# Rank-2 additions of a two-step pair placed in four row groups of the array, in a feed-forward with repeated weights

## What is computed

```python
def _qlora_linear(x, wq, A, B):          # rank r = 2, scaling 0.5
    w = jnp.tile(wq, (1, 4))
    return x @ w.T + x @ A.T @ B.T * LORA_SCALING
...
s = silu(x @ w_gate.T)                   # first feed-forward, I = 2752
# the half of each token's s with the smallest absolute value is set to zero
x = _layernorm(x + (s * (x @ w_up.T)) @ w_down.T)
...
gate = jax.nn.silu(_qlora_linear(x, w1q, a1, b1))    # second feed-forward
up = _qlora_linear(x, w3q, a3, b3)
return _layernorm(x + _qlora_linear(gate * up, w2q, a2, b2))
```

## Time and profile before

| | |
|---|---|
| median of three runs | 2139.07 us |
| the profiled execution | 2140.85 us |
| its span in the profile | 2139.1 us |
| TensorE matmul (PE) busy | 2047.8 us, 96%, 11008 matmuls |
| weight loads (PEld) busy | 1824.7 us, 85% |
| VectorE (DVE) busy | 1110.8 us, 52% |
| ScalarE (ACT) busy | 782.3 us, 37% |
| GpSimd (POOL) busy | 1055.7 us, 49% |
| mean granted clock of TensorE | 0.975 |

### The profile page before, as it was taken

One profiled execution on the slowest core, in us unless ns is written; L12 is line 12 of the kernel. 1 busy time (PEld: TensorE's weight loads), 2 busy tenths in 40 slices (PEclk: granted clock), 3 DMA queues, 4 the chain that ended last, 5 costly groups with the idle time before them and its releaser, 6 DMA issues.

```text
span 2139.1 us, 32155 instructions
## 1 busy us (share of the span) xinstructions
PE 2047.8 (96%) x11008; PEld 1824.7 (85%) x11008; DVE 1110.8 (52%) x1818; ACT 782.3 (37%) x1280; POOL 1055.7 (49%) x740
## 2 busy tenths in 40 slices
PE   8997959999999999999999999999998999999998
PEld 8997949978899998889999888998776777777776
DVE  1146773368965345896633488652025354354543
ACT  3245333355233334623232372322243415244251
POOL 6445744435444543454454345443575727366281
PEclk9998979989999998999999899999999999999999
DMA  4332313323443332344343234334431403314130
GB/s 132 93 94 66 104 44 92 93 72 97 137 127 110 109 93 70 97 138 126 88 132 93 70 95 140 108 111 139 132 121 46 157 30 124 102 49 147 50 127 40
DMA packets 90366, 213.63 MB, mean 100 GB/s; under 512 B 10360, under 2 KB 12408, under 8 KB 89188
## 3 DMA queue, kind: packets, MB, share of 16 engines
q1 hardware_dynamic: 85616, 194.97, 30.1%
q10 hardware_dynamic: 4608, 16.78, 2.0%
HBM read 194.93 MB, written 16.78 MB: 99 GB/s over the span
## 4 chain that ended last, share of the span: by engine, by line
issue 38%; PE 32%; POOL 25%; ACT 2%; DMA 1%; DVE 1%; POOLq 1%; SPq 0%; DVEq 0%; ACTq 0%
POOL wl L463 18%; PE bank L1277 10%; PE bank L1278 10%; PE bank L1279 10%; POOL w13l L463 3%; POOL h2l L561 2%; POOL xTl L463 1%; PE bank L1448 1%; PE bank L1410 1%; ACT junka L663 1%; POOL hql L567 1%; DMA w_in_place<-in_wd 1%; PE bank L1401 0%; PE bank L1420 0%; DMA w_in_place<-in_wu 0%
## 5 line engine op out<-in xcount | busy, mean ns | idle before, releaser
L463 POOL TENSOR_TENSOR wl<-w_in_place,wh 128x688 fp32r<-128x688 f32 (+1 forms) x432 | 676.5, 1568 | 795.8 <-ACT wh L604 795.6
L1277 PE MATMUL bank<-wh,xTh 128*128 128x344 f32 x2048 | 661.5, 323 | 31.5 <-POOL wl L463 15.6
L1279 PE MATMUL bank<-wh,xTl 128*128 128x344 f32 x2048 | 658.6, 322 | 0.0
L1278 PE MATMUL bank<-wl,xTh 128*128 128x344 f32 x2048 | 657.3, 321 | 0.0
L604 ACT CAST wh<-w_in_place 128x688 fp32r<-128x688 f32 (+1 forms) x432 | 305.1, 706 | 872.0 <-DMA w_in_place<-in_wu 310.9
L1277 PEld LDWEIGHTS bank<-wh,xTh 128*128 128x128 f32 x2048 | 388.2, 190 | 34.4 <-issue 21.0
L1278 PEld LDWEIGHTS bank<-wl,xTh 128*128 128x128 f32 x2048 | 388.4, 190 | 0.0
L1279 PEld LDWEIGHTS bank<-wh,xTl 128*128 128x128 f32 x2048 | 387.9, 189 | 0.0
L1277 PE MATMUL bank<-wh,hTh 128*128 128x512 f32 (+1 forms) x704 | 284.6, 404 | 12.2 <-ACT v L633 6.4
L1278 PE MATMUL bank<-wl,hTh 128*128 128x512 f32 (+1 forms) x704 | 282.9, 402 | 0.0
L1279 PE MATMUL bank<-wh,hTl 128*128 128x512 f32 (+1 forms) x704 | 282.5, 401 | 0.0
(11 more groups left out here) (130 smaller groups left out, 2456.0 us busy)
## 6 DMA issues: line engine op xcount, KB each, us to landing
w_in_place<-in_wg SPq DMA_DIRECT2D x128, 344.0 KB, 3.0
w_in_place<-in_wu SPq DMA_DIRECT2D x128, 344.0 KB, 3.0
w_in_place<-in_wd SPq DMA_DIRECT2D x168, 256.0 KB, 2.6
w_in_place<-in_w SPq DMA_DIRECT2D x90, 256.0 KB, 3.6
x_in_place<-in_xT SPq DMA_DIRECT2D x32, 256.0 KB, 3.5
y<-in_xtok SPq DMA_DIRECT2D x4, 2048.0 KB, 8.5
x<-y ACTq DMA_DIRECT2D x16, 512.0 KB, 3.5
xa<-x SPq DMA_DIRECT2D x16, 512.0 KB, 4.8
```

Source lines behind the costliest of these rows:

```text
L463: nc.gpsimd.tensor_tensor(lo, landed, hi.bitcast(F32), ALU.subtract).then_inc(done, 1)
L1277: nc.tensor.matmul(dst, ah, bh, start=start, stop=False)
L1278: nc.tensor.matmul(dst, ah, bl, start=False, stop=False)
L1279: return nc.tensor.matmul(dst, al, bh, start=False, stop=stop)
```

## The change

The four rank-2 additions of two steps (gate and up of each) become four matmuls that contract over six rows each, at rows 0, 32, 64 and 96, in four banks. Each group of six rows holds what the 96-row form held in three places: `b` high with `x` high, the low part of the one with the high part of the other, and the reverse. For this `a13s` gets 102 columns, so that bank 7 holds all the copies; `braw` gets all the copies of `b1` and `b3`; two masks of one column each, `split_b` and `split_x`, turn copies into high or low parts. The steps run in pairs: base matmuls of step m0 and m0 + 1, then the four additions, then the four `low_h` matmuls of the pair before. ScalarE and GpSimd follow the same order. The last pair's `low_h` moves into `down_2`, behind five chunks of both halves of group 0. `t2s` moves in memory.

```diff
@@ load_b, SyncE @@
                 for g in range(3):
-                    for i, (src, c0) in enumerate(((b1, 0), (b3, 0), (b2, IB), (b2, IB))):
-                        r0 = 32 * g + R * (i % 2)
-                        sp.dma_start(braw[r0:r0 + R, c0:c0 + src.shape[1]], src).then_inc(b_in, 16)
+                    for i, src in enumerate((b1, b3, b1, b3)):
+                        r0 = UP * i + R * g
+                        sp.dma_start(braw[r0:r0 + R, 0:IB], src).then_inc(b_in, 16)
+                    for i in range(2):
+                        r0 = 32 * g + R * i
+                        sp.dma_start(braw[r0:r0 + R, IB:IB + H], b2).then_inc(b_in, 16)
@@ GpSimd, last down @@
                 if d == 4:
...
-                    nc.gpsimd.memset(keep[:], 1.0).then_inc(pool_s, 1)
...
+                    for part, new, old, n in ((split_b, (LORA, -1.0), (0.0, 1.0), 2 * R), (split_x, (1.0, -1.0), (0.0, 1.0), R)):
+                        for i in range(2):
+                            fill(part[:, i:i + 1], old[i])
+                            for p0 in QUAD:
+                                fill(part[p0:p0 + n + R, i:i + 1], new[i])
+                                fill(part[p0:p0 + n, i:i + 1], old[i])
+                    pool.sem_inc(split_ready, 1)
                     nc.gpsimd.memset(t2s[0:LR, :].bitcast(F32), 0.0).then_inc(keep_ready, 1)
...
-                if d == 28:
...
-                    nc.gpsimd.memset(lg[0:LR, :].bitcast(F32), 0.0).then_inc(keep_ready, 1)
-                    nc.gpsimd.memset(lu[0:LR, :].bitcast(F32), 0.0).then_inc(keep_ready, 1)
@@ steps_2, GpSimd @@
-                for m in range(STEPS):
+                for m in range(0, STEPS, 2):
                     c, q, _ = place(m)
                     if c < CQ - 1:
                         low_13(b, c + 1, q)
-                    if m:
-                        low_h(m - 1)
+                        low_13(b, c + 1, q + 1)
                     if q == 0 and c:
                         low_q(c - 1)
-                    if m == 5:
+                    low_h(m)
+                    low_h(m + 1)
+                    if m == 4:
                         inv_std(NB + b - 1)
-                low_h(STEPS - 1)
                 low_q(CQ - 1)
@@ steps_2, ScalarE @@
+                for m in range(0, STEPS, 2):
+                    c, q, rows = place(m)
+                    if c < CQ - 1:
+                        high_13(b, c + 1, q)
+                        high_13(b, c + 1, q + 1)
+                    silu(m)
+                    silu(m + 1)
                     if q == 0 and c:
                         high_q(c - 1)
+                    high_h(m)
+                    high_h(m + 1)
@@ VectorE, preparation @@
             dve.wait_ge(b_ready, 2)
-            V.scalar_tensor_tensor(out=b13[64:LR, :], in0=braw[64:LR, 0:IB], scalar=LORA,
-                                   in1=b13[64:LR, :].bitcast(F32), op0=ALU.mult, op1=ALU.subtract).then_inc(b_ready, 1)
+            dve.wait_ge(split_ready, 1)
+            step(V.tensor_scalar(braw[0:LX, 0:IB], braw[0:LX, 0:IB], split_b[0:LX, 0:1], None, ALU.mult))
+            st.done()
+            V.scalar_tensor_tensor(out=b13[0:LX, :], in0=b13[0:LX, :].bitcast(F32), scalar=split_b[0:LX, 1:2],
+                                   in1=braw[0:LX, 0:IB], op0=ALU.mult, op1=ALU.add).then_inc(b_ready, 1)
@@ low_rank_x, VectorE @@
-                step(V.tensor_copy(th[0:n, :], banks[7][0:n, :]))
+                step(V.tensor_copy(lx[0:LX, :], banks[7][0:LX, :]))
+                step(V.tensor_scalar(rest[0:LX, :], banks[7][0:LX, :], split_x[0:LX, 0:1], None, ALU.mult))
                 st.done()
-                step(V.tensor_tensor(tl[0:n, :], banks[7][0:n, :], th[0:n, :].bitcast(F32), ALU.subtract))
-                st.done()
-                for i, dst in enumerate((lg, lu)):
-                    for p0, src in ((0, th), (32, tl), (64, th)):
-                        step(V.tensor_scalar(dst[p0:p0 + n, :], src[0:n, :].bitcast(F32), keep[0:n, i:i + 1], None,
-                                             ALU.mult))
+                step(V.scalar_tensor_tensor(out=lx[0:LX, :], in0=lx[0:LX, :].bitcast(F32), scalar=split_x[0:LX, 1:2],
+                                            in1=rest[0:LX, :], op0=ALU.mult, op1=ALU.add))
@@ steps_2, TensorE @@
+                for m0 in range(0, STEPS, 2):
...
+                    for m in (m0, m0 + 1):
...
+                        for i in range(2):
+                            dst = banks[2 * (m - m0) + i][0:rows, :]
+                            if m >= 2:
+                                pe.wait_ge((s_done, h_done)[i], STEPS * b + m - 1)
...
+                    for m in (m0, m0 + 1):
+                        mm = slice(c * Q4 * P + place(m)[1] * rows, c * Q4 * P + (place(m)[1] + 1) * rows)
+                        for i, done in enumerate((gg_done, uu_done)):
+                            p0 = QUAD[2 * (m - m0) + i]
+                            nc.tensor.matmul(banks[2 * (m - m0) + i][0:rows, :], b13[p0:p0 + 3 * R, mm],
+                                             lx[p0:p0 + 3 * R, :], start=False, stop=True).then_inc(done, 1)
+                    if m0:
+                        low_h(b, m0 - 2, q + 2 == steps_of(c))
+                        low_h(b, m0 - 1, False)
@@ down_2, TensorE @@
                 if t == 0:
+                    pe.wait_ge(h_done, STEPS * b + STEPS - 1)
...
+                    for n in range(2):
+                        for c in range(CQ - 1):
+                            add(n, c)
+                        if n == 0 and between is not None:
+                            between()
+                    low_h(b, STEPS - 2, False)
+                    low_h(b, STEPS - 1, False)
+                    pe.wait_ge(ql_done, CQ * (b + 1))
...
+                    for n in range(2):
+                        add(n, CQ - 1)
```

More of the change, by code:

```diff
@@ L1428, in steps_2 @@
                 pe.wait_ge(l_ready, b + 1)
-                for m in range(STEPS):
-                    c, q, rows = place(m)
+                for m0 in range(0, STEPS, 2):
+                    c, q, rows = place(m0)
                     if q == 0:
@@ L1455, in down_2, with add @@
+            def down_2(b, t, between=None):
+                tt = slice(t * P, (t + 1) * P)
+                def add(n, c):
+                    rows, w = rows_of(c), slice(n * 512, (n + 1) * 512)
+                    three(banks[2 * (t % 2) + n][:, :], hqh[0:rows, c, tt], hql[0:rows, c, tt], w2h[0:rows, c, w],
+                          w2l[0:rows, c, w], c == 0, False)
                 if t == 0:
+                    pe.wait_ge(h_done, STEPS * b + STEPS - 1)
+                    pe.sem_inc(passed_pe, 1)
@@ new lines, in down_2 @@
+                    low_h(b, STEPS - 2, False)
+                    low_h(b, STEPS - 1, False)
+                    pe.wait_ge(ql_done, CQ * (b + 1))
+                    pe.sem_inc(passed_pe, 1)
+                    for n in range(2):
+                        add(n, CQ - 1)
+                else:
+                    if t >= 2:
+                        pe.wait_ge(e_evac, 2 * NT * b + 2 * (t - 1))
+                        pe.sem_inc(passed_pe, 1)
+                    for n in range(2):
+                        for c in range(CQ):
+                            add(n, c)
+                        if n == 0 and between is not None:
+                            between()
```

96 lines of the change are left out of this document (35 added, 61 removed).

## The result

The changed kernel takes 2157.18 us (median of four runs, 2156.33 to 2160.12) against 2139.64 (four runs of the kernel before beside it, 2138.78 to 2142.1): a ratio of 1.0083, with a 95% interval of 1.0065 to 1.0100. It is 17.5 us slower, where 5.7 were forecast. The profiled executions are 2160.12 and 2140.85 us, with spans of 2158.3 and 2139.1, so the profiles differ by 19.2.

A forecast was written before the change was run, and what follows sets the result against it. TensorE was taken as the bound, GpSimd close behind. Four blocks -1.7, `down_2` +5.0, `low_rank_x` -2.4 and -0.7, last `down` +5.55 sum to +5.75 us on 2139.07: 2144.8 us, range 2132 to 2155.

The forecast's parts named there:

- d: How late the first of a pair's four additions starts on TensorE; taken as 0.17 us, between 0 and 0.26.
- Q: Time from a pair's first addition to its first `low_h` on TensorE; taken as 0.45 us, between 0.24 and 0.8.
- A's clean share: Rival: the additions share the array at no extra cost (d = 0, Q = 0.24), total 2138.7 us; chance 0.27.
- D's serial loads: Rival: the additions' loads follow one another and the array empties twice (Q = 0.8), total 2155.3 us; chance 0.11.
- E: Rival: the four additions run one after another (Q = 0.93), total 2149.7 us; chance 0.08.
- The pair and the chunk: Second feed-forward: a free pair of steps takes 7.12 us, chunks 2 and 3 14.87 each, limited by GpSimd's chain.
- T: Start of a pair's additions on TensorE, from which the prediction counted its times in us.
- Chunk 1: Normalization of the block before delays the second product and the root adds 1.0 us; next chunk at T + 10.9.
- `down_2`: Last two `low_h` stand later, so the rank-2 addition waits 1.24 us for `t2s`, four times: +5.0 us.
- `low_rank_x`: Three operations replace eight: TensorE's wait at block 0 falls from 4.86 to 2.45 us, -2.4; other three borders -0.7.
- The last `down`: First feed-forward's preparation: fills +1.65 us, six more transfers +1.8, a longer pass over `braw` +2.1; together +5.55.
- Rival C: TensorE stays the bound throughout, 44 pairs x 3 slots = -30.6 us, total 2116 us; chance 0.05.

The follow-up runs named there:

- one_group: The changed kernel with all four additions of a pair reading rows 0 to 5, so three add the wrong part: 2161.92 us, one run.
- stats_early: The changed kernel with layer-norm sums taken within the first two chunks and GpSimd's inverse root at step 6, ahead of that pair's low parts: 2141.26 us, ratio 0.9998.
- wait_3: stats_early with GpSimd writing zeros over zeros in `t2s` twice, ahead of `w13l` for chunk 2, as a deliberate delay: 2162.19 us, ratio 1.0087.
- lowh_mid: The changed kernel with a block's last two `low_h` moved between the halves of the first tile of `down_2`: 2153.61 us, ratio 1.0054.
- before_18: The kernel before the change with 18 transfers for b instead of 12, the six more to rows nothing reads: 2148.97 us, ratio 1.0038.
- root_only: The changed kernel with only GpSimd's inverse root moved to step 6, VectorE's sums left in steps 1 to 4: 2147.68 us, ratio 1.0032.
- prep_spread: The changed kernel with its 18 transfers for b in three groups of six, ahead of pieces 23, 25 and 26: 2152.36 us, ratio 1.0047.
- all_moves: The changed kernel with the edits of hq_first, lowh_mid, stats_early and prep_spread together: 2118.24 us, ratio 0.9891.
- hq_first: The changed kernel with ScalarE's `high_q` ahead of the pair's two Silus instead of behind them: 2151.79 us, ratio 1.0050.

## Why the prediction was wrong

The sign and the main mechanism were right: TensorE gains by the additions, GpSimd's chain of each pair takes it back. The size was wrong, 17.5 us instead of 5.7, and beyond the range's end of 2155.

1. **The additions** (d = 0.17, Q = 0.45 forecast): 0.09 and 0.43 to 0.44. Right; A's clean share (Q = 0.24), D's serial loads (0.8) and E fell; one_group shows additions that do run one after another (Q = 1.13). From the last base matmul to the first `low_h` five slots, 1.16 us, became 0.76. The Trainium skill, TensorE: Matmul & The Clock Gate, Part 3, gives 3.07x for four tiles; here it is 0.93 us against the record's 0.50 or Q's 0.44, 1.9x to 2.1x; Q is 0.2 us more than a slot.
2. **The pair and the chunk** (7.12 and 14.87): a free pair takes 6.92 us, 0.08 of the difference by the smaller d, the rest by the slots: 0.227 us among the 24 base matmuls, where 0.232 was taken. The next pair starts at T + 1.37 as forecast, because of Q and four `low_h`; bank 0 alone would let it start at T + 1.28 (the first pair of a block). Chunks 2 and 3 take 14.84 to 14.89: there GpSimd's chain was read to the tenth of a microsecond.
3. **Chunk 1** (16.64 forecast): 17.19 where the clock stayed up (block 1), 18.9 to 19.9 in the three others. This is the step that failed: "the next chunk starts at T + 10.9" priced the wait as a wait (the chunk started at T + 11.6 to 11.7), 0.55 us short, and nothing for what TensorE's clock does behind it. It was in view: the same fall stands in the earlier trace rows, and I weighed it only at the start of block 0. It cost 8.3 us over the four blocks (74.88 against 66.56), 2.2 as waiting and 6.1 by the clock. stats_early removes all of it and the forecast stall too, and wait_3 brings it back with another cause, 7.0 us of clock for 10.9 of waiting.
4. **`down_2`**: +5.0 for `t2s` was right (lowh_mid: 1.2 each). The wait for `hql` at its start was missed: `high_q` behind both Silus was put into the chunks' chain but not followed to its last user, `down_2`'s first matmul behind only four `low_h`. 1.22, 1.22, 1.23 and 2.09 us, 5.8, against 0.7 counted (as a wait for bank 0 in the last block), and in the last block some 1.6 us of clock (from its start to the end of the span 46.9 us in the changed kernel, 45.3 in stats_early, where the same wait of 2.10 left the clock up).
5. **`low_rank_x`** (-2.4): the wait fell from 5.50 to 4.07, although the cast to `xsh` ahead of the new operations took 1.20 us where it took 0.29 before. The stage as a whole gained nothing: in this run its first tile took 5.8 us and the others 4.1 (1606.88, 1612.64, 1616.73), with the granted clock at 0.65 from 1608 to 1612. Of the eleven profiles with the new operations five read 22.3 us for the stage, as this one, and six read 20.6, with all four tiles at 4.1: the gain is 1.7 us when the clock is up. At the three other borders the forecast held: from the last matmul of `down_2` to the first step it is 0.22 us less.
6. **The last `down`** (+5.55, measured +5.2): right only in the sum. The fills took 5.5 us, not 6.5, and TensorE waited 0.38, not 1.65; piece 30 waited 0.25, not 2.5, although the products on `braw` stretched three subtractions to 8.56 us (1561.69; 7.13 in the kernel before); piece 22 waited 5.78, not 4.7, and the clock was 0.50 for six microseconds behind it. before_18 gives the price of six transfers alone: 3.5 us of waiting and the clock, against my 1.8. They delay the weights by more than the queue's issue time. And the forecast's 5.55 was all waiting, where half of the 5.2 is the clock.

Points 3 and 4 come to 15.0 us over the forecast (8.3, 5.1 and 1.6), yet the four blocks stand only 9.2 over it (+11.8 against +2.6): shorter pairs, and first additions 5.54 us into the block instead of 5.74 in three blocks, hid part of the miss, and the rest isn't taken apart. Another 2.1 of the 19.2 between the profiles lie in code that the change doesn't touch.

What stays open: which waits bring the clock down. Behind 1.32 (one_group, block 2), 1.56 (root_only, block 0) and 1.90 us (prep_spread) it fell, behind 1.33 (one_group, block 1), 2.97 (changed kernel, block 1), 3.05 (all_moves) and 2.10 us (stats_early, last `down_2`) it did not; behind the four of 3.44 to 3.60 it always did. Of the sixteen waits of 2.96 to 3.00 us at chunk 2 in the profiles of the changed kernel, hq_first, lowh_mid and prep_spread, thirteen brought it down. No run separates the length from what TensorE did ahead of it.

Rival C, 2116 us with TensorE the bound throughout, had 0.05. all_moves is 2 us from it, though not by its terms: from the first step on it is 20.7 us under the kernel before where C has 26.3, and its last `down` is 1.1 longer where C counts 5.55. What the change lacked was an order of the other engines' work that lets TensorE keep most of what it gains.

## What to carry to other kernels

When work is taken off the engine that sets the pace, follow every producer that stands behind a moved instruction to its last user, statistics and stage ends included; the next-slowest engine's order decides whether the gain arrives, and here a change of order alone was worth 39 to 41 us. Price a new wait of TensorE twice, once as itself and once with the clock that it may cost (1.4 to 2.9 us where it fell, behind waits of 1.3 to 3.6 us in the blocks here), and give both ends to the range. A step may move earlier or be grouped, but look what leaves after it: statistics and output tiles four steps later made TensorE wait 9 us for its next loads.

## What the runs showed of the hardware

- Four matmuls over six rows each, at rows 0, 32, 64 and 96 and in four banks, have one record of 0.50 us; at the same rows they take 1.20. In both cases the first starts 0.09 late, and the next matmul over 128 rows about 0.2.
- The granted clock can fall to 0.50 behind a wait of 1.32 us and stay up behind one of 3.05, so the same program differs from block to block, which may be why root_only's ten runs are spread over 2143.85 to 2153.7 (only one of them has a profile).
- 36 fills of one column with a wait each take 0.15 us apiece (2.63 us for 18).
- Six more transfers of two rows each made TensorE's wait for the next weights 3.5 us longer, though the queue is busy with them for 1.7 us only (1.14 us for four in the last `down` above).
- A VectorE product over 102 rows of 2784 columns takes 4.03 us, and three subtractions on GpSimd beside it and its neighbours took 8.56 us instead of 3.9.
